# One four-tile burst for masked scores times values, in place of two two-tile bursts, in a vision-tower kernel

## The chip, the cores and the metric

The kernel runs on one core of one Trainium2 chip. The metric is device time in microseconds (us); lower is better. The engines are TensorE (PE, with its weight loads shown apart as PEld), VectorE (DVE), ScalarE (ACT), GpSimd (POOL) and SyncE (SP), which issues the DMAs. They run side by side and meet at semaphores.

## The reference

The input is `x` of shape (128, 64, 64, 64). Three stages follow one another:

- *Tokens.* Each 4x4 patch of pixels is averaged to one token of 64 channels; a small attention (8 heads) of that token over its 16 pixels is added.
- *Attention.* Linear attention with decay, 8 heads of width 8, in chunks of 128 tokens:

```
scores = einsum('bhcd,bhed->bhce', qi, ki) * mask
intra  = einsum('bhce,bhed->bhcd', scores, vi)
inter  = einsum('bhcd,bhde->bhce', qi * q_dec, S)
```

  `mask` is the decay matrix, zero above the diagonal, and `S` the state carried from one chunk to the next. The output is `intra + inter`, projected, added and normalised.
- *Experts.* A router chooses 2 of 8 small MLPs per token; their sum is added and normalised.

The change touches `intra` alone.

## The kernel before

Two images are laid side by side on the 128 partitions (64 channels each), and half of their pixels make one *unit*: 128 tokens of two images, so 16 (image, head) pairs in one tile of 128 x 128. There are 128 units. The first two stages are a software pipeline written out by hand: each engine runs a function `step(i, r)` for unit `4 i + r`, and a step works on several units at once, each at another stage (`there(i, r, lag)` says whether the unit `lag` steps back exists). The parity `s = r % 2` chooses one of two buffers, and the state `S` is used in odd steps alone. Most of the steps run in a hardware loop. Each engine executes its own list in program order; a `wait_ge` stops the list of its engine until a semaphore has the given count.

In one step TensorE computes, for the newest unit, four pixel rows each of keys (`keys(j)`, L342 and L347, tiles of 64x64) and values (`values(j)`, L366, whole array); for the unit one step back, sums over a head (`selected()`, L317 and L320, four column tiles of 128x32); for older units the projections and the attention. `queries()` (L377) and `queries_turned()` (L385) prepare the queries of the next unit; between them ScalarE (L568 to L584) and VectorE (L818 to L825) compute a norm. Everything here is f32, and one f32 matmul shows as two matmul records and two weight loads.

Attention of the unit four steps back: `scores(f)` (L412) computes queries times keys, for half `f` of the 16 pairs, into PSUM banks 3 and 4. VectorE multiplies them by the mask into `sm` (L763, masks 0 and 1 after `scores(0)`, masks 2 and 3 after `scores(1)`). `attend(f)` (L427) applies them to the values: the group `g` of four pairs goes to column tile `g` of the array, that is to partitions 32 g to 32 g + 31 of PSUM bank 7, and its four pairs add up there, because `vpad` holds each pair's values with zeros in the other pairs' columns. `attend(0)` handles groups 0 and 1, eight matmuls in the order jj outer, g inner, so that two column tiles take turns; `attend(1)` does groups 2 and 3 the same way at the end of the step. In odd steps L434 adds the state's part. Then `o_done` lets ScalarE evict the result (L529), and `attended()` (L455) of the next step projects it.

The wait functions matter for the order: `keys_free(j)` stands ahead of `keys(j)` and waits until VectorE (L752) and ScalarE (L517) have read the keys of row j - 1. ScalarE's list in the middle of a step is: L555 to L563 (values and tokens out of PSUM), `values(1)` (L524), L568 to L584. VectorE's is: L752 for row 1, L800 to L810, L818 to L825, L752 for row 2, the softmax steps L835 to L844, masks 2 and 3, L752 for row 3.

Of the kernel before, what the change touches and what calls it, by code (L numbers as in the profile page):

```python
# [13 lines left out]
def vit_tower_kernel(nc, x, ln_q_w, ln_q_b, Wq, ln_kv_w, ln_kv_b, Wkv, proj_w, proj_b,  # L14
                     w_qkv, w_proj, b_proj, slopes, router_w, w1, b1, w2, b2, out):
    P = 128
# [19 lines left out]
    def done(i, r, lag, per, plus=0):  # L36

        if isinstance(i, int):
            return max(0, max(0, min(UNITS, 4 * i + r - lag + 1)) * per + plus)
        return i * (4 * per) + (r - lag + 1) * per + plus  # L40

    def there(i, r, lag):
        return not isinstance(i, int) or 0 <= 4 * i + r - lag < UNITS

    def pairs(i, r, back, per=1):

        if isinstance(i, int):
            return max(0, min(UNITS // 2, 2 * i + r // 2 + back)) * per
        return i * (2 * per) + (r // 2 + back) * per
# [14 lines left out]
    def units(eng, step):  # L64

        step(-1, 2)
        step(-1, 3)
        for i in (0, 1):
            for r in range(4):
                step(i, r)  # L70
        with eng.Fori(2, UNITS // 4 - 1) as i:
            for r in range(4):
                step(i, r)
        for u in range(UNITS - 4, UNITS + 6):
            step(u // 4, u % 4)

    with ExitStack() as ctx:
# [3 lines left out]
        def sem(name):  # L81
            return ctx.enter_context(nc.semaphore(name))
# [10 lines left out]
        B7 = ps[:, 7, :]  # L93
# [27 lines left out]
        with ExitStack() as early:  # L121
            def sb1(name, shape, dt=F32):
                return early.enter_context(nc.sbuf_tensor(name, shape, dt))
# [57 lines left out]
            qdm = sb1("qdm", [P, P])  # L181
            sblk = sb1("sblk", [P, P])
# [49 lines left out]
            vk_ev = sem("vk_ev")  # L232
# [3 lines left out]
            sb_done = sem("sb_done")  # L236
            qd_done = sem("qd_done")
            qm_done = sem("qm_done")
            sc_done = sem("sc_done")
            mask_done = sem("mask_done")  # L240
            o_done = sem("o_done")
            oT_done = sem("oT_done")
            pr_done = sem("pr_done")
            lt_done = sem("lt_done")
# [51 lines left out]
            def _(pe):  # L296
# [8 lines left out]
                def step(i, r):  # L305
                    s = r % 2
# [45 lines left out]
                    def keys_free(j):  # L352

                        if there(i, r, 0):
                            if j == 0:
                                pe.wait_ge(x_in[r], 16 * NL * (i + 1))
                            pe.wait_ge(kq_done, done(i, r, 1, ST, j))
                            pe.wait_ge(cs_done, done(i, r, 1, ST, j))

                    def values(j):  # L360

                        if there(i, r, 0):
                            pe.wait_ge(vs_done, done(i, r, 1, ST, j))
                            xv = xb[:, r, :].rearrange("p (b t d) -> p b d t", b=ST, d=ST)
                            for b in range(ST):
                                mm = nc.tensor.matmul(VB[:, b * P:(b + 1) * P], xv[:, b, j], w_ckv[:, P:2 * P],  # L366
                                                      start=True, stop=True)
                            mm.then_inc(v_pe, 1)
# [43 lines left out]
                                nc.tensor.matmul(SCB[g % 2], kT[hp, s, :], qm[hp, s, :],  # L412
                                                 start=True, stop=True).then_inc(sc_done, 1)

                    def attend(f):

                        if not there(i, r, 4):
                            return
                        if f == 0:
                            pe.wait_ge(lt_done, done(i, r, 5, 1))  # L420
                            pe.wait_ge(sb_done, pairs(i, r, -2 + s))
                            pe.wait_ge(vk_ev, done(i, r, 4, 2))
                        pe.wait_ge(mask_done, done(i, r, 5, 4, 2 * f + 2))
                        for jj in range(4):
                            for g in (2 * f, 2 * f + 1):
                                at = g * 4 * VW + jj * W
                                mm = nc.tensor.matmul(B7[g * W:(g + 1) * W, 0:P], vpad[:, s, at:at + W],  # L427
                                                      sm[:, (4 * g + jj) * P:(4 * g + jj + 1) * P], start=(jj == 0),
                                                      stop=(jj == 3 and s == 0))
                        if f == 1:  # L430
                            if s == 1:

                                pe.wait_ge(qd_done, pairs(i, r, -1))
                                mm = nc.tensor.matmul(B7[:, 0:P], sblk[:], qdm[:], start=False, stop=True)  # L434
                            mm.then_inc(o_done, 1)

                    def aggregated():

# [6 lines left out]
                    def projected():  # L445
                        if there(i, r, 2):
                            pe.wait_ge(agT_ev, done(i, r, 2, 1))
                            nc.tensor.matmul(B6[:, P:2 * P], w_pj[:], aggT[:], start=True,
                                             stop=True).then_inc(pj_done, 1)
# [25 lines left out]
                    keys(1)  # L475
                    attn_vk()
                    values(1)
                    attend(0)
                    keys_free(2)
                    queries()  # L480
                    keys(2)
# [5 lines left out]
                    aggregated()  # L487
                    values(3)
                    projected()
                    attend(1)  # L490
                units(pe, step)

            @block.scalar
# [850 lines left out]
```

## Time and profile before

| | us |
|---|---|
| median of 3 runs | 3491.15 (3491.13 to 3492.43) |
| the profiled execution | 3490.56 |
| its span in the profile | 3488.5 |
| TensorE busy | 3308.4 (95%) |
| VectorE, GpSimd, ScalarE busy | 2025.1, 1746.6, 1488.5 |

The pipeline of the first two stages runs from about 46 us to about 2874 us, the routing and the experts after it. A time is the start of an instruction, counted from the start of the span. A row of the order of time merges neighbouring instructions of a line: its length goes from the first start to the last end. Matmuls overlap in that view, since a matmul's end is modelled, so the distance between starts of rows is what a group costs.

### The profile page before, as it was taken

The numbers are of one execution on the slowest core, as the hardware profiler recorded it, in microseconds if no ns is written. First come the engines' busy times: TensorE is split into PE (matmuls) and PEld (weight loads), VectorE is DVE, ScalarE is ACT, GpSimd is POOL, SyncE is SP. The second block draws the span as 40 slices with busy tenths as digits, with TensorE's granted clock in tenths as the row PEclk, the third lists the DMA queues.
The fourth block names the chain that finished last, engine by engine and source line by source line (L and its number), as shares of the span: only waits on it lengthen the run. The fifth ranks groups of instructions, "written<-read, shape, count | busy, mean of one in ns | idle before, by whom it ended". The sixth has DMA issues, their size and how long they took to land. (4 is left out here: it accounts for less than half of the span.)

```text
span 3488.5 us, 68919 instructions
## 1 busy us (share of the span) xinstructions
PE 3308.4 (95%) x21221; PEld 2063.2 (59%) x21221; DVE 2025.1 (58%) x4349; ACT 1488.5 (43%) x4493; POOL 1746.6 (50%) x1789
## 2 busy tenths in 40 slices
PE   4999999999999999999999999999999976399998
PEld 2666666666666666666666666666666646244333
DVE  3566666666666666666666666666666650655554
ACT  2444444444444444444444444444444433244443
POOL 2655555555555555555555555555555530011211
PEclk9999999999999999999999999999999975599999
DMA  3322222222222222222222222222222100000000
GB/s 65 61 50 49 48 48 48 48 48 48 48 48 48 48 48 48 48 48 48 48 48 48 48 48 48 48 48 48 48 48 48 25 1 5 0 19 18 18 21 21
DMA packets 573517, 144.09 MB, mean 41 GB/s; under 512 B 573472, under 2 KB 573472, under 8 KB 573472
## 3 DMA queue, kind: packets, MB, share of 16 engines
q1 hardware_dynamic: 573472, 143.51, 21.3%
q8 instruction: 25, 0.41, 0.1%
q14 instruction: 20, 0.16, 0.0%
HBM read 135.08 MB, written 8.39 MB: 41 GB/s over the span
## 5 line engine op out<-in xcount | busy, mean ns | idle before, releaser
L366 PEld LDWEIGHTS ps<-w_ckv,xb 128*128 128x128 f32 x4096 | 1008.2, 327 | 218.1 <-issue 192.1
L366 PE MATMUL ps<-w_ckv,xb 128*128 128x128 f32 x4096 | 1048.1, 399 | 0.9 <-DVE kqs L752 0.8
L636 POOL TENSOR_TENSOR pv<-vs,aw 128x512 f32<-128x512 f32 x512 | 534.7, 1077 | 668.5 <-DVE aw L854 365.8
L524 ACT ACTIVATE vs<-ps 128x512 f32<-128x512 f32 x512 | 305.7, 597 | 848.8 <-PE ps L366 848.8
L342 PE MATMUL ps<-xb,w_ckv 64*64 64x512 f32 x2048 | 553.4, 617 | 0.0
L347 PE MATMUL ps<-xb,w_ckv 64*64 64x512 f32 x2048 | 553.3, 617 | 0.0
L752 DVE TENSOR_TENSOR kqs<-ps,qqT 128x512 f32<-128x512 f32 x512 | 350.9, 685 | 332.9 <-PE ps L347 332.9
L763 DVE TENSOR_TENSOR sm<-ps,decay 128x512 f32<-128x512 f32 x512 | 328.7, 683 | 155.2 <-PE ps L412 155.2
L517 ACT ACTIVATE sqs<-ps 128x512 f32<-128x512 f32 x512 | 304.7, 595 | 211.8 <-PE ps L347 211.8
L666 POOL TENSOR_TENSOR xt<-xb 128x512 f32<-128x512 f32 x256 | 325.3, 1292 | 20.3 <-issue 19.9
L643 POOL TENSOR_TENSOR pv<-pv 128x512 f32<-128x512 f32 x256 | 323.1, 1284 | 0.0
L412 PE MATMUL ps<-qm,kT 32*128 32x512 f32 x1024 | 292.3, 647 | 0.0
L427 PE MATMUL ps<-sm,vpad 128*32 128x128 f32 x4096 | 278.0, 279 | 9.5 <-DVE sm L763 9.5
L656 POOL TENSOR_TENSOR htok<-htok,bp_row 128x128 f32<-128x128 f32 x128 | 58.3, 456 | 424.0 <-ACT htok L563 424.0
L1287 DVE TENSOR_TENSOR hid<-ps,hid 128x512 f32<-128x512 f32 x256 | 162.5, 685 | 156.2 <-PE ps L1080 150.4
L800 DVE TENSOR_REDUCE agg<-pv 128x128 f32<-128x1024 f32 x128 | 248.2, 1939 | 0.6 <-POOL pv L643 0.6
L427 PEld LDWEIGHTS ps<-sm,vpad 128*32 128x32 f32 x4096 | 207.8, 111 | 47.4 <-DVE sm L763 10.1
L1187 ACT ACTIVATE hid<-ps,b1p 128x1024 f32<-128x1024 f32 x128 | 142.5, 1114 | 195.8 <-PE ps L1069 195.8
L782 DVE TENSOR_TENSOR lt<-ps,htok 128x128 f32<-128x128 f32 x128 | 37.3, 291 | 272.0 <-PE ps L462 136.7
L818 DVE SCALAR_TENSOR_TENSOR ps<-ps,y0s 128x48 f32<-128x48 f32 x136 | 29.4, 216 | 275.6 <-ACT y0s L584 275.6
L977 POOL TENSOR_TENSOR y<-y 128x512 f32<-128x512 f32 x32 | 33.2, 1039 | 268.2 <-ACT y L1200 268.2
L669 POOL TENSOR_TENSOR xt<-xt 128x512 f32<-128x512 f32 x128 | 162.2, 1267 | 10.0
(222 smaller groups left out, 4899.9 us busy)
## 6 DMA issues: line engine op xcount, KB each, us to landing
xb<-in_x_dram SPq DMA_DIRECT2D x512, 256.0 KB, 4.3
out_dram<-outb SPq DMA_DIRECT2D x128, 64.0 KB, 1.6
w1p<-in_L_ffn_w_dram SPq DMA_DIRECT2D x16, 16.0 KB
b2v<-in_L_ffn_b_dram SPq DMA_DIRECT2D x16, 2.0 KB
w2p<-in_L_ffn_w_dram SPq DMA_DIRECT2D x8, 16.0 KB
b1p<-in_L_ffn_b_dram SPq DMA_DIRECT2D x8, 0.2 KB
sm<-in_L_tok_Wkv_dram SPq DMA_DIRECT2D x4, 16.0 KB, 2.0
w_avki<-in_L_attn_w_qkv_dram SPq DMA_DIRECT2D x4, 16.0 KB, 2.8
```

Source lines behind the costliest of these rows:

```text
L342: nc.tensor.matmul(KB[own, :], w_ckv[own, 2 * P + m * C:2 * P + (m + 1) * C], xv[own, j], start=True, stop=True)
L347: mm = nc.tensor.matmul(CB[(1 - m) * C:(2 - m) * C, :], w_ckv[own, m * C:(m + 1) * C], xv[own, j], start=True, stop=True)
L366: mm = nc.tensor.matmul(VB[:, b * P:(b + 1) * P], xv[:, b, j], w_ckv[:, P:2 * P], start=True, stop=True)
L412: nc.tensor.matmul(SCB[g % 2], kT[hp, s, :], qm[hp, s, :], start=True, stop=True).then_inc(sc_done, 1)
L427: mm = nc.tensor.matmul(B7[g * W:(g + 1) * W, 0:P], vpad[:, s, at:at + W], sm[:, (4 * g + jj) * P:(4 * g + jj + 1) * P], start=(jj == 0), ...
L517: nc.scalar.activation(sqs[:, j, :], CB, ACT.Square).then_inc(cs_done, 1)
L524: nc.scalar.activation(vs[:, s, j * 4 * P:(j + 1) * 4 * P], VB, ACT.Copy).then_inc(vs_done, 1)
L636: nc.gpsimd.tensor_tensor(pv[:, at].rearrange("p (k d) -> p k d", d=D), vs[:, s, at].rearrange("p (k d) -> p k d", d=D), aw[:, j * W4:(j + ...
L643: nc.gpsimd.tensor_tensor(pv[:, j * 4 * P:(j + 1) * 4 * P], pv[:, j * 4 * P:(j + 1) * 4 * P], pv[:, (j + 2) * 4 * P:(j + 3) * 4 * P], ALU. ...
L666: ins = nc.gpsimd.tensor_tensor(xt[:, h * H:(h + 1) * H], xb[:, f, h * H:(h + 1) * H], xb[:, f, (h + 2) * H:(h + 3) * H], ALU.add)
L752: V.tensor_tensor(kqs[:, j, :].rearrange("p (t d) -> p t d", d=ST), KB.rearrange("p (t d) -> p t d", d=ST), qqT[:, s, :].unsqueeze(2).to_b ...
L763: V.tensor_tensor(sm[:, g * 512:(g + 1) * 512].rearrange("p (h c) -> p h c", c=P), SCB[g % 2].rearrange("p (h c) -> p h c", c=P), decay[:, ...
```

## The change

`attend(f)` becomes `attend()`. It issues all sixteen matmuls in one burst, at the place of the old `attend(1)`, in the order jj outer, g inner, so that four column tiles take turns. The call between `values(1)` and `keys_free(2)` goes away. The wait for `sb_done` is now made in odd steps only, ahead of L434. Operands, shapes, addresses and the sums themselves stay.

```diff
-                    def attend(f):
+                    def attend():
 
                         if not there(i, r, 4):
                             return
-                        if f == 0:
-                            pe.wait_ge(lt_done, done(i, r, 5, 1))
-                            pe.wait_ge(sb_done, pairs(i, r, -2 + s))
-                            pe.wait_ge(vk_ev, done(i, r, 4, 2))
-                        pe.wait_ge(mask_done, done(i, r, 5, 4, 2 * f + 2))
+                        pe.wait_ge(lt_done, done(i, r, 5, 1))
+                        pe.wait_ge(vk_ev, done(i, r, 4, 2))
+                        pe.wait_ge(mask_done, done(i, r, 5, 4, 4))
                         for jj in range(4):
-                            for g in (2 * f, 2 * f + 1):
+                            for g in range(4):
                                 at = g * 4 * VW + jj * W
                                 mm = nc.tensor.matmul(B7[g * W:(g + 1) * W, 0:P], vpad[:, s, at:at + W],
                                                       sm[:, (4 * g + jj) * P:(4 * g + jj + 1) * P], start=(jj == 0),
                                                       stop=(jj == 3 and s == 0))
-                        if f == 1:
-                            if s == 1:
+                        if s == 1:
 
-                                pe.wait_ge(qd_done, pairs(i, r, -1))
-                                mm = nc.tensor.matmul(B7[:, 0:P], sblk[:], qdm[:], start=False, stop=True)
-                            mm.then_inc(o_done, 1)
+                            pe.wait_ge(sb_done, pairs(i, r, -2 + s))
+                            pe.wait_ge(qd_done, pairs(i, r, -1))
+                            mm = nc.tensor.matmul(B7[:, 0:P], sblk[:], qdm[:], start=False, stop=True)
+                        mm.then_inc(o_done, 1)
...
                     values(1)
-                    attend(0)
                     keys_free(2)
...
                     projected()
-                    attend(1)
+                    attend()
```

## Rows read from the trace of the kernel before

**Rows 1.** The page: busy time by engine, and the group of L427.
```profile
PE 3308.4 (95%) x21221; PEld 2063.2 (59%) x21221; DVE 2025.1 (58%) x4349; ACT 1488.5 (43%) x4493; POOL 1746.6 (50%) x1789
...
L427 PE MATMUL ps<-sm,vpad 128*32 128x128 f32 x4096 | 278.0, 279 | 9.5 <-DVE sm L763 9.5
```
**Rows 2.** Stages: window, its length, busy us (instructions) by engine, granted clock, DMA.
```profile
1534.04:1535.04 1.00, 1.00 (x23) 1.00 (x26) 0.91 (x3) 0.56 (x1) 0.59 (x1) 1.00 0.00 0
...
1513.55:1513.65 0.10, 0.10 (x5) 0.10 (x8) 0.00 (x0) 0.00 (x0) 0.10 (x1) 1.00 0.62 143
137.60:2770.00 2632.40, 2632.40 (x17194) 1703.91 (x17197) 1620.26 (x3454) 1163.04 (x3874) 1567.00 (x1574) 1.00 0.25 48
...
1503.91:1525.81 21.90, 21.90 (x144) 14.07 (x142) 13.51 (x29) 9.44 (x31) 13.24 (x14) 1.00 0.25 48
1525.81:1547.40 21.59, 21.59 (x145) 14.07 (x143) 13.22 (x30) 9.77 (x33) 12.66 (x14) 1.00 0.25 49
```
**Rows 3.** TensorE in order of time, an odd step: start us, length us.
```profile
1501.08 1.90 PE L366 MATMUL ps<-w_ckv,xb 128*128 128x128 f32 x8
1502.91 1.07 PE L427 MATMUL ps<-sm,vpad 128*32 128x128 f32 x16
1503.91 0.70 PE L377 MATMUL ps<-w_qc,red 128*128 128x256 f32 x2
1504.54 0.65 PE L342 MATMUL ps<-xb,w_ckv 64*64 64x512 f32 x2
...
1505.56 1.13 PE L412 MATMUL ps<-qm,kT 32*128 32x512 f32 x4
1506.62 2.13 PE L366 MATMUL ps<-w_ckv,xb 128*128 128x128 f32 x8
1508.59 0.27 PE L385 MATMUL ps<-ident,q 128*128 128x128 f32 x1
...
1512.13 1.07 PE L427 MATMUL ps<-sm,vpad 128*32 128x128 f32 x16
```
**Rows 4.** TensorE in order of time, in the ramp, before attention has begun.
```profile
112.52 1.90 PE L366 MATMUL ps<-w_ckv,xb 128*128 128x128 f32 x8
114.25 0.60 PE L377 MATMUL ps<-w_qc,red 128*128 128x256 f32 x2
114.78 0.65 PE L342 MATMUL ps<-xb,w_ckv 64*64 64x512 f32 x2
...
118.76 0.33 PE L385 MATMUL ps<-ident,q 128*128 128x128 f32 x1 [0.82 <-DVE kqs L752]
```
**Rows 5.** TensorE in order of time: four column tiles, and one whole-array tile.
```profile
1513.55 1.06 PE L317 MATMUL ps<-kqs,selk 128*32 128x512 f32 x8
...
3207.72 1.08 PE L1088 MATMUL ps<-tokT,centre 128*128 128x512 f32 x2
```
**Rows 6.** TensorE in order of time, end of an even step.
```profile
1534.04 0.74 PE L427 MATMUL ps<-sm,vpad 128*32 128x128 f32 x10
1534.52 0.62 PE L317 MATMUL ps<-kqs,selk 128*32 128x512 f32 x2
...
1536.76 0.49 PE L455 MATMUL ps<-w_ap,oT 128*128 128x128 f32 x2
```
**Rows 7.** ScalarE and VectorE in order of time, the same odd step.
```profile
1503.02 0.60 ACT L524 ACTIVATE vs<-ps 128x512 f32<-128x512 f32 x1 [0.95 <-PE ps L366]
1504.64 0.28 ACT L568 ACTIVATE qps<-ps 128x128 f32<-128x128 f32 x1 [1.03 <-PE ps L377]
...
1507.79 0.68 DVE L752 TENSOR_TENSOR kqs<-ps,qqT 128x512 f32<-128x512 f32 x1
...
1510.38 1.28 DVE L763 TENSOR_TENSOR sm<-ps,decay 128x512 f32<-128x512 f32 x2
```
**Rows 8.** TensorE in order of time, in the drain.
```profile
2849.49 1.92 PE L427 MATMUL ps<-sm,vpad 128*32 128x128 f32 x16
2851.34 2.08 PE L412 MATMUL ps<-qm,kT 32*128 32x512 f32 x4
```

## The prediction

> **What bounds the kernel now.** Read the busy line first: TensorE is busy 95% of the span, twice any DMA share and well above VectorE's 58% [rows 1]. A busy TensorE can still be waiting, because matmul ends are modelled, so I went to the stages next. From 137.6 to 2770 us its busy time equals the window, at granted clock 1.00, and VectorE, ScalarE and GpSimd stand at 62%, 44% and 60% [rows 2]. Two neighbouring steps take 21.90 and 21.59 us; each has about 144 matmul records and as many weight loads, two records per f32 matmul [rows 2]. Then the order of time inside a step: each group of matmuls starts where the one before ends, with no idle time named in front of it [rows 3]. So in 124 of the 128 steps with an `attend` pair TensorE's own work sets the pace, and what is cut there comes off the span, until an engine that feeds it becomes late.
>
> **What a burst costs.** The 4096 records of L427 are 256 bursts of 16, two per unit [rows 1]. A burst's row is 1.07 us long and one record lasts 0.27 us, so first and last start lie 0.80 us apart. The burst goes round two column tiles, so a tile starts 8 records in 0.80 us: one about every 0.11 us, first included. The two tiles run beside each other. The question of the change is whether four do.
>
> The nearest rows say yes. L317 goes round four column tiles of the same shape of weights (128x32) with 512 columns in place of 128: its 8 records take 1.06 us from the first start to the last end [rows 5]. L1088, one tile of the whole array with 512 columns, takes 1.08 us for 2 records [rows 5]. Eight on four tiles cost what two cost on one, so all four stream at once. A round of L427 at four tiles is then taken as long as at two, 0.11 us, plus a stagger of about 0.01 us for the two added tiles. New burst: 0.81 us between first and last start, with twice the matmuls. Bounds: 0.80 us (no stagger at all) from below, 1.6 us (each record still costs 0.80/15 = 0.053 us, as at two tiles, 31 intervals) from above. I take 0.81 because L317 is the nearest row in tiles and type; the 1.6 us stays for the range.
>
> **The change part by part.**
> 1. *The first burst goes from between `values(1)` and `queries()`.* Now L427 starts at 1502.91, L377 at 1503.91 and the next `keys` (L342) at 1504.54 [rows 3]. L366's eight records start at 1501.08 in the same step, 3.46 us ahead of that L342, and 1.83 us ahead of L427. The trace of before holds the form of after too: in the ramp, before the first unit has reached attention, L366 is followed directly by L377. There L366 starts at 112.52, L377 at 114.25, L342 at 114.78: 2.26 us [rows 4]. Ramp form: 1.73 us from L366 to L377 and 0.53 from L377 to L342. Present form: 1.83 + 1.00, and 0.63. The edit saves (1.83 + 1.00 + 0.63) - 2.26 = 1.20 us per step. Of it 0.80 is the burst, the rest are the two changes of the tile shape around it, and a weight load of L377 that the end of L366 hides. Nothing covers or uncovers this; both forms are on record at full clock.
> 2. *Its eight matmuls go into the last burst.* +0.01 us by the working above. In an even step the old last burst used tiles 2 and 3 only, and L317 of the next step already starts 0.48 us into it [rows 6]. That could have been an overlap that the change loses. It isn't: tiles 2 and 3 must run 8 records and then their share of L317 and L320, and only their end counts; tiles 0 and 1 just finish earlier. With four tiles full, the longest tile does the same work. So 0 lost; the other bound is 0.4 us (the whole head start lost), in even steps alone, 0.2 us per step on average.
> 3. *Waits.* `sb_done` is now waited for only ahead of L434, in odd steps. The VectorE multiply that gives it follows `lt` near the start of a step, some 10 us earlier: 0. The merged wait for `mask_done` is the one that the second burst had: masks 2 and 3 end at 10.38 + 1.28 = 1511.66, and L427 starts at 1512.13 [rows 3, 7], 0.47 us of slack. Behind that wait stand L434 and the next step's `selected()`, as now: 0.
> 4. *What is late next.* The removed 1.20 us were cover for whatever runs from the first half of a step into the second. The tight one is the chain behind `queries()`: L377, ScalarE L568 to L584, VectorE L818 to L752, then L385, which stands behind `keys_free(3)`. Now L752 ends at 1507.79 + 0.68 = 1508.47 and L385 starts at 1508.59 [rows 3, 7]: only 0.12 us, about what a wait takes to pass. The matmuls between L377 and L385 stay, so this distance only shrinks by the 0.10 us of item 1 on both sides. But L568 also follows ScalarE's eviction L524, which ends at 1503.02 + 0.60 = 1503.62, while L568, at 1504.64 now, would be due at 1503.44 [rows 7]. It will be some 0.1 us late, in an odd step, where the chain is longest. The ramp shows such a wait: L385 with 0.82 us idle in front, for VectorE L752 [rows 4], in a step that lacks the `scores(1)` of a full step, 1.06 us from L412 at 1505.56 to L366 at 1506.62 [rows 3]: 0.82 is less than 1.06, so it confirms that the chain nearly fits. I take 0.05 us per step; bounds 0 and 0.3 us (VectorE and ScalarE slowed by each other's nearness as well).
>    The other engines have 21.6 us for 13.5, 12.7 to 13.2 and 9.8 us of work [rows 2] and can follow a step of 20.6. The x loads need a quarter of the DMA time [rows 2].
>
> Per full step: 1.20 - 0.01 - 0.05 = 1.14 us. Times 124: 141.4 us. The last four pairs lie in the drain at half clock or behind VectorE. Two of them (one from 2849.49 to 2851.34 [rows 8]) have the burst of 1.85 us ahead of `scores(1)` on the path, so 3.7 us; two wait for VectorE's long chain anyway, 0. **Sum:** 145 us. The profiled execution takes 3490.56 us (span 3488.5), 0.6 below the median of the runs shown: 3490.6 - 145 = 3345.5, as a median 3346 us. The stages after 2874 us don't change.
>
> **The rivals.**
> *A. The instructions come too slowly.* The burst is now 32 matmul records and 32 weight loads that should start in 0.81 us, 13 ns each. The fullest microsecond of the trace, 1534.04 to 1535.04, has 22 to 23 matmuls and 26 loads starting [rows 2], 20 ns each. If 20 ns is a limit, the burst lasts 1.3 us: +0.5 per step, 3346 + 62 = 3408. If a record costs 0.053 us as at two tiles, +0.8 per step: 3449. For it: no stretch with 128 columns on four tiles exists. Against: within 1513.55 to 1513.65 four tiles start 8 loads and 4 to 5 matmuls in 0.1 us [rows 2], so at least in the short the pace is there, and in the 1534 window tiles 0 and 1 were occupied by L317's long records, so that work and not supply limited the count. Chance 0.10.
> The Trainium skill, page "TensorE: Matmul & The Clock Gate", section "Wait — 56ns, not 53.3ns?", states that with hardware decode off the sequencer spends about 62 ns on each matmul, which binds where the array needs less. By that rule 32 records would take 1.98 us, an estimate from the page, and the time would come to about 3490; the two-tile burst with its 53 ns per record [rows 3] is a little faster than the rule allows, though a filled queue could explain that.
> *B. The cover is missing more than I think.* The chain of item 4 stops L385 for 0.3 us per step: 3346 + 37 = 3383. For it: 0.12 us of slack [rows 3, 7]. Against: ramp steps whose idle time is below what `scores(1)` fills. Chance 0.07.
> *C. Slower.* Half of the doubled burst (32 instructions, what a burst needs today) is ready in the queue, the others arrive at the mean pace of a step, 286 in 21.90 us or 77 ns each [rows 2]. The burst then takes 0.44 + 32 x 0.077 = 2.9 us, 2.1 more than now, against 1.20 saved: +0.9 per step, 3490.6 + 112 = about 3600. The sign turns where an instruction needs more than (0.81 + 1.14 - 0.44)/32, or 47 ns. The 1534 window with 20 ns speaks against it. Chance 0.03.
>
> **How the numbers follow.** Forecast 0.80, A 0.10, B 0.07, C 0.03. The forecast's own range is 3336 (no stall, the drain a little shorter) to 3364 (0.15 us per step left behind somewhere). With B and the milder half of A the range is 3336 to 3400. About 0.2% (7 us) is what this kernel's runs can tell from nothing: faster by more 0.95, within it 0.02 (a pace between A's worst and C's), slower 0.03.
>
> **What would show each step.** Right: L427 with 128 bursts of 32 records, first to last start 0.8 us; L366 followed by L377 1.73 us after its start in every step; step lengths of about 20.4 and 20.75 us; L385 with at most 0.1 us idle, behind VectorE L752. A shows as a longer L427 row at the same count; B as idle time at L385 or L342 with VectorE or ScalarE as the releaser; a lost overlap as a longer way from L427 to L455 in even steps (now 2.72 us, from 1534.04 to 1536.76 [rows 6]). The prediction is wrong if steps don't shorten by more than 1 us though TensorE keeps its full clock.

## The result and the profile after

The changed kernel takes 3358.89 us (median of 4 runs, 3357.21 to 3360.96) against 3491.14 us for the kernel before on the same chip: ratio 0.9622, 95% interval 0.9605 to 0.9638. The forecast was 3346 us, range 3336 to 3400 us: right in sign and range, 13 us too low. All the kernels below were timed beside the kernel before, whose medians (3491.14, 3490.50 and 3490.51 us) agree within 0.7 us, so their times can be compared with each other. The profiled execution took 3357.21 us, span 3355.2. Line numbers after the edit are two or three lower than before (L427 is L425, L752 is L749, L825 is L822); those up to L412 stay.

The page of the changed kernel, its busy line and the group of the burst:

```profile
PE 3167.0 (94%) x21221; PEld 1953.0 (58%) x21221; DVE 2052.1 (61%) x4349; ACT 1474.8 (44%) x4493; POOL 1748.5 (52%) x1789
...
L425 PE MATMUL ps<-sm,vpad 128*32 128x128 f32 x4096 | 141.8, 280 | 7.4 <-DVE sm L760 7.4
```

The records are as many as before [rows 1], each as long (280 against 279 ns), and yet the group's busy time is half: 141.8 for 278.0 us. Busy time counts a moment once, so twice as many records now lie on top of each other.

The stages, with the columns of rows 2:

```profile
137.60:2640.00 2502.40, 2497.16 (x17167) 1596.50 (x17166) 1642.86 (x3440) 1148.43 (x3871) 1567.44 (x1571) 1.00 0.26 50
1498.04:1518.68 20.64, 20.61 (x143) 13.23 (x143) 13.54 (x30) 9.66 (x33) 12.69 (x14) 1.00 0.27 51
1518.68:1539.40 20.72, 20.72 (x143) 13.20 (x143) 13.73 (x29) 9.33 (x31) 13.27 (x14) 1.00 0.26 51
```

The first short window runs from L377 of an even step to the next L377, the second is the odd step after it. The even step took 21.59 us [rows 2] and takes 20.64 now, the odd one took 21.90 and takes 20.72. In the even step TensorE is no longer busy all the time (20.61 of 20.64). VectorE's busy time there has grown from 13.22 us [rows 2] to 13.54 with no instruction added, which is the hint to what follows.

TensorE in order of time: the second half of an even step with its burst, then the same of the odd step after it:

```profile
1500.65 2.13 PE L366 MATMUL ps<-w_ckv,xb 128*128 128x128 f32 x8
1502.81 0.33 PE L385 MATMUL ps<-ident,q 128*128 128x128 f32 x1
1503.07 0.65 PE L342 MATMUL ps<-xb,w_ckv 64*64 64x512 f32 x2
...
1506.41 1.08 PE L425 MATMUL ps<-sm,vpad 128*32 128x128 f32 x32
1507.31 1.04 PE L317 MATMUL ps<-kqs,selk 128*32 128x512 f32 x8
...
1509.14 0.49 PE L453 MATMUL ps<-w_ap,oT 128*128 128x128 f32 x2
...
1516.94 1.90 PE L366 MATMUL ps<-w_ckv,xb 128*128 128x128 f32 x8
1518.68 0.60 PE L377 MATMUL ps<-w_qc,red 128*128 128x256 f32 x2
1519.21 0.65 PE L342 MATMUL ps<-xb,w_ckv 64*64 64x512 f32 x2
...
1521.29 2.13 PE L366 MATMUL ps<-w_ckv,xb 128*128 128x128 f32 x8
1523.26 0.27 PE L385 MATMUL ps<-ident,q 128*128 128x128 f32 x1
1523.46 0.65 PE L342 MATMUL ps<-xb,w_ckv 64*64 64x512 f32 x2
...
1526.81 1.08 PE L425 MATMUL ps<-sm,vpad 128*32 128x128 f32 x32
1527.82 0.49 PE L432 MATMUL ps<-qdm,sblk 128*128 128x128 f32 x2
```

Three things are to be seen. The burst has 32 records in a row of 1.08 us, where 16 took 1.07 [rows 3]. L366 to L377 to L342 takes 1.74 + 0.53 us, the form that the ramp showed [rows 4]. And L385 follows L366 after 1.97 us in the odd step, but after 2.16 us in the even one, and L342 another 0.26 in place of 0.20 us later. The same holds over the steady part of the trace. The even steps take 20.64 and 20.75 us in turns, where experiment 1 below has 20.39, so they lose 0.25 or 0.36 us; the odd ones take 20.72 us and lose nothing. That is 0.153 us per step. The forecast had named 20.4 and 20.75 us: the odd step came as forecast, the even one did not.

What L385 waits for, in the group of its weight loads (idle time and releaser at the end), in the kernel before (137.6 to 2770 us) and after (137.6 to 2640 us):

```profile
L385 PEld LDWEIGHTS ps<-ident,q 128*128 128x128 f32 x122 | 23.1, 190 | 0.0
```
```profile
L385 PEld LDWEIGHTS ps<-ident,q 128*128 128x128 f32 x120 | 16.6, 138 | 16.7 <-DVE kqs L749 16.7
```

Two explanations were set against each other. Theory P: VectorE's multiply that makes q2 (L822) now meets an addition of GpSimd. Theory S: ScalarE's part of the chain (L565 to L581) starts too late behind its eviction L521.

### The profile page after: what moved, and what is told of

Read it like the earlier page. It is cut to its first block and busy times, and to the rows that moved or that the text cites. A ratio compares the mean times of both kernels' runs of the same rounds, so it can differ in the third digit from the quotient of the medians.

```text
span 3355.2 us, 68942 instructions
## 1 busy us (share of the span) xinstructions
PE 3167.0 (94%) x21221; PEld 1953.0 (58%) x21221; DVE 2052.1 (61%) x4349; ACT 1474.8 (44%) x4493; POOL 1748.5 (52%) x1789
## 5 line engine op out<-in xcount | busy, mean ns | idle before, releaser
L366 PEld LDWEIGHTS ps<-w_ckv,xb 128*128 128x128 f32 x4096 | 1008.0, 327 | 217.0 <-issue 189.7
L366 PE MATMUL ps<-w_ckv,xb 128*128 128x128 f32 x4096 | 1047.9, 399 | 0.9 <-DVE kqs L749 0.8
L521 ACT ACTIVATE vs<-ps 128x512 f32<-128x512 f32 x512 | 305.7, 597 | 839.4 <-PE ps L366 839.4
L749 DVE TENSOR_TENSOR kqs<-ps,qqT 128x512 f32<-128x512 f32 x512 | 350.6, 685 | 330.6 <-PE ps L347 330.6
L342 PE MATMUL ps<-xb,w_ckv 64*64 64x512 f32 x2048 | 552.1, 616 | 0.0
L663 POOL TENSOR_TENSOR xt<-xb 128x512 f32<-128x512 f32 x256 | 325.4, 1292 | 20.4 <-issue 20.0
L412 PE MATMUL ps<-qm,kT 32*128 32x512 f32 x1024 | 292.3, 647 | 2.9 <-DVE sm L760 2.2
L530 ACT ACTIVATE ssb<-ps 128x512 f32<-128x512 f32 x128 | 76.4, 597 | 194.5 <-PE ps L320 194.5
L342 PEld LDWEIGHTS ps<-xb,w_ckv 64*64 64x64 f32 x2048 | 99.8, 131 | 92.9 <-issue 46.4
L425 PE MATMUL ps<-sm,vpad 128*32 128x128 f32 x4096 | 141.8, 280 | 7.4 <-DVE sm L760 7.4
```

Of the source, the lines that this page charges most:

```text
L342: nc.tensor.matmul(KB[own, :], w_ckv[own, 2 * P + m * C:2 * P + (m + 1) * C], xv[own, j], start=True, stop=True)
L412: nc.tensor.matmul(SCB[g % 2], kT[hp, s, :], qm[hp, s, :], start=True, stop=True).then_inc(sc_done, 1)
L521: nc.scalar.activation(vs[:, s, j * 4 * P:(j + 1) * 4 * P], VB, ACT.Copy).then_inc(vs_done, 1)
L663: ins = nc.gpsimd.tensor_tensor(xt[:, h * H:(h + 1) * H], xb[:, f, h * H:(h + 1) * H], xb[:, f, (h + 2) * H:(h + 3) * H], ALU.add)
L749: V.tensor_tensor(kqs[:, j, :].rearrange("p (t d) -> p t d", d=ST), KB.rearrange("p (t d) -> p t d", d=ST), qqT[:, s, :].unsqueeze(2).to_b ...
```

## The experiments

All are variants of the changed kernel, but the last, which is one of the kernel before; times are medians, ratios against the kernel before.

**1. GpSimd's order.** The additions of x go ahead of the one on `htok`; the last of them, `red`, stays where it was.

```diff
-                        pool.wait_ge(vk_ev, done(i, r, 3, 2))
-                        nc.gpsimd.tensor_tensor(htok[:, o, :], ..., ALU.add).then_inc(hb_done, 1)
                     if there(i, r, -2):
...
                         link(nc.gpsimd.tensor_tensor(xp[:, 0:2, :], xp[:, 0:2, :], xp[:, 2:4, :], ALU.add))
+                    if there(i, r, 3):
+                        pool.wait_ge(vk_ev, done(i, r, 3, 2))
+                        nc.gpsimd.tensor_tensor(htok[:, o, :], ..., ALU.add).then_inc(hb_done, 1)
+                    if there(i, r, -2):
                         pool.wait_ge(qp_pe, done(i, r, -1, 1))
```

> The changed kernel, with GpSimd's additions of x moved ahead of its addition on htok; red stays last. Theory P (port): in the changed kernel VectorE's multiply that makes q2 (L822) meets GpSimd's L668 in the even steps and takes 0.82 us in place of 0.42 us, so L385 starts 0.26 to 0.37 us late there, 0.155 us per step. With GpSimd done before q2 begins, L822 should take 0.42 us in both parities, L385 should follow L366 after 0.23 us, a step takes 20.56 us, and the time is 3358.9 - 19 = 3340 us. Rival S (ScalarE): the chain is late because L565 follows the eviction L521 more closely than before; then L385 stays late and the time stays at 3359 us.

Measured: 3340.17 us (3338.69 to 3342.10), ratio 0.9569 (0.9553 to 0.9584), as theory P had it to within a microsecond. VectorE and GpSimd in order of time in an even step of the changed kernel, then the same with TensorE in an even step of this one:

```profile
1501.34 0.82 DVE L822 TENSOR_SCALAR q<-qps,yrs 128x64 f32<-128x64 f32 x2
1502.08 0.68 DVE L749 TENSOR_TENSOR kqs<-ps,qqT 128x512 f32<-128x512 f32 x1
...
1501.40 0.71 POOL L668 TENSOR_TENSOR xt<-xt 128x256 f32<-128x256 f32 x1
```
```profile
1534.20 0.42 DVE L824 TENSOR_SCALAR q<-qps,yrs 128x64 f32<-128x64 f32 x2
...
1530.30 0.67 POOL L665 TENSOR_TENSOR xt<-xt 128x256 f32<-128x256 f32 x1
1531.05 0.46 POOL L668 TENSOR_TENSOR htok<-htok,bp_row 128x128 f32<-128x128 f32 x1
1532.62 0.41 POOL L673 TENSOR_TENSOR red<-xt 128x128 f32<-128x128 f32 x1 [1.11 <-ACT h L570]
...
1533.43 2.13 PE L366 MATMUL ps<-w_ckv,xb 128*128 128x128 f32 x8
1535.40 0.27 PE L385 MATMUL ps<-ident,q 128*128 128x128 f32 x1
```

In the changed kernel q2's two small multiplies overlap GpSimd's L668 and end 0.05 us after it, at 1502.16; with GpSimd out of the way they take half the time, and L385 is back at 1.97 us behind L366, in all even steps. Theory S is out: ScalarE's L565 starts 0.69 to 0.77 us after L377 in the changed kernel and in this one alike, and the stall is there in the one and gone in the other. The group of L385's weight loads has lost its idle time:

```profile
L385 PEld LDWEIGHTS ps<-ident,q 128*128 128x128 f32 x120 | 23.9, 199 | 0.0
```

The same multiply, mean ns of one of its two instructions, in the steady stage of before, changed, experiment 1:

```profile
L825 DVE TENSOR_SCALAR q<-qps,yrs 128x64 f32<-128x64 f32 x244 | 63.8, 303 | 4.4
```
```profile
L822 DVE TENSOR_SCALAR q<-qps,yrs 128x64 f32<-128x64 f32 x240 | 80.7, 378 | 4.3
```
```profile
L824 DVE TENSOR_SCALAR q<-qps,yrs 128x64 f32<-128x64 f32 x240 | 50.2, 252 | 4.3
```

The move takes other meetings away too. VectorE's multiply for `kd`, which runs in odd steps beside GpSimd's first additions of x, falls from 1.35 us to 0.28:

```profile
L809 DVE TENSOR_TENSOR kd<-kpl,kdec 128x128 f32<-128x128 f32 x60 | 16.7, 278 | 0.0
```

This does not bear on the even steps, which have no such multiply; in the one shown VectorE had idled 1.74 us for ScalarE ahead of the chain.

**2. VectorE's order.** The third row of keys goes ahead of the chain that makes q2.

```diff
+                    keys(2)
                     link, n = chain(dve, newt_ch, (4 * i + r + 2) * 3)
...
                         ins.then_inc(q2_done, 1)
-                    keys(2)
```

> The changed kernel, with VectorE's product of the third row of keys (L749) moved ahead of the chain L815 to L822, into the 1.74 us in which VectorE now waits for ScalarE in even steps. L385 waits for both. Theory P and any theory in which the chain up to L749 is too long: in even steps q2 ends 0.68 us sooner counted to L385, so L385 is no longer late although L822 may still meet GpSimd; in odd steps L749 then ends when it did. 3340 us (3338 to 3345). If it was not this chain that held L385: 3359 us.

Measured: 3356.33 us (3355.64 to 3356.94), ratio 0.9614 (0.9598 to 0.9630): a miss by 16 us. The expectation held for the even steps and failed for the odd ones. TensorE in this kernel, an even step and the next odd one, then VectorE and GpSimd in the odd one:

```profile
1499.54 2.13 PE L366 MATMUL ps<-w_ckv,xb 128*128 128x128 f32 x8
1501.51 0.27 PE L385 MATMUL ps<-ident,q 128*128 128x128 f32 x1
...
1519.92 2.13 PE L366 MATMUL ps<-w_ckv,xb 128*128 128x128 f32 x8
1522.14 0.30 PE L385 MATMUL ps<-ident,q 128*128 128x128 f32 x1
...
1518.39 1.35 DVE L807 TENSOR_TENSOR kd<-kpl,kdec 128x128 f32<-128x128 f32 x1
1519.67 0.68 DVE L749 TENSOR_TENSOR kqs<-ps,qqT 128x512 f32<-128x512 f32 x1
...
1521.00 0.89 DVE L823 TENSOR_SCALAR q<-qps,yrs 128x64 f32<-128x64 f32 x2
...
1521.03 0.65 POOL L668 TENSOR_TENSOR xt<-xt 128x256 f32<-128x256 f32 x1
```

In an odd step VectorE has no free time there (L807 runs until 1519.74), so the moved product only pushes q2 later, into GpSimd's L668: L823 takes 0.89 us, and L385 comes 2.22 us after L366. L807 itself is long because it runs beside GpSimd (0.28 us in experiment 1). The stall has changed parity: an even step now takes 20.39 us and an odd one 21.00, so 0.31 us lost in even steps have become 0.27 us in odd ones.

**3. ScalarE's order.** `values(1)` goes behind the chain that ends with `y0s`.

```diff
-                    values(1)
                     if there(i, r, -1):
...
                     nc.scalar.activation(y0s[:], y0[:], ACT.Square).then_inc(rs_ch, 1)
+                    values(1)
                     centred(2)
```

> The changed kernel, with ScalarE's eviction values(1) (L521) moved behind the chain L565 to L581. Rival S: L565 starts as soon as L377 ends and L385 is no longer late, 3340 us. Theory P: L565 gains at most 0.1 us (it starts 0.70 us after L377, and 0.66 at best in the ramp), which shifts q2 by 0.1 us against GpSimd; L822 still meets L666 or L668 and the stall stays in the main: 3350 to 3362 us.

Measured: 3411.31 us (3406.80 to 3413.13), ratio 0.9770 (0.9754 to 0.9787), outside both expectations. The eviction now comes too late for `values(2)`, here in an odd step:

```profile
1509.96 1.13 PE L412 MATMUL ps<-qm,kT 32*128 32x512 f32 x4
1511.42 2.13 PE L366 MATMUL ps<-w_ckv,xb 128*128 128x128 f32 x8 [0.33 <-ACT vs L521]
1513.39 0.27 PE L385 MATMUL ps<-ident,q 128*128 128x128 f32 x1
```

L366 starts 0.4 us later than the 1.06 us after L412 that it needs, and L385, now reached later, no longer waits. So this run does not tell the two theories apart; experiment 1 does. It shows that the step has a second place with little cover. Against experiment 1 it costs 71 us. Most steps are 0.4 to 0.5 us longer, some 52 us in 124. Another 15 us come from TensorE's clock: 14 of the steps took 21.8 to 22.2 us, and in each of them the granted clock fell to 0.5 (1.2 GHz) for a stretch (mean 0.92 over the step), as it does in no steady step of the changed kernel or of experiment 1. In one of them, 1486.48 to 1508.41, TensorE had idled 0.41 us ahead of L366 before the clock fell at 1491.5. Why these 14 steps and not the others, which idle there too, no run shows.

**4. Both moves, 1 and 2.**

> Both the GpSimd move and the VectorE move. If either alone removes the wait before L385, both together give the same, 3340 us, since TensorE then has no wait left: L385 follows L366 after 0.23 us in every step and a step takes 20.56 us. A further gain of over 3 us would show a wait that the profile does not name.

Measured: 3339.91 us (3339.40 to 3340.52), ratio 0.9568 (0.9552 to 0.9584), the same as experiment 1. With GpSimd's additions out of the way, VectorE's order is worth nothing.

**5. One burst, two tiles at a time.** The place stays, the order of the two old bursts comes back.

```diff
-                        for jj in range(4):
-                            for g in range(4):
+                        for g0, jj in [(0, 0), (0, 1), (0, 2), (0, 3), (2, 0), (2, 1), (2, 2), (2, 3)]:
+                            for g in (g0, g0 + 1):
```

> The changed kernel with one burst at the same place, but in the order of the two old bursts: first the eight matmuls of groups 0 and 1 in turns, then the eight of groups 2 and 3. This is the kernel before with its first burst moved, and without four tiles in turns. Theory T (tiles run side by side only where their instructions stand near each other in the list): in the kernel before L317 on tiles 0 and 1 began when 10 of the 32 instructions of a burst on tiles 2 and 3 were still to start, 0.47 us into it. So the second half starts 0.47 us after the first, the burst lasts about 1.27 us from first to last start in place of 0.81, a step gets 0.46 us longer: 3358.9 + 57 = 3416 us. Rival N (no overlap over a longer distance than the neighbour): 1.7 us, +0.87 us per step, 3467 us. Rival F (TensorE sorts freely within its queue, or the whole gain came from the removed changes of tile shape): no difference, 3359 us.

Measured: 3417.65 us (3414.22 to 3418.19), ratio 0.9792 (0.9775 to 0.9808). Theory T (tiles run side by side only where their instructions stand near each other in the list) holds within 2 us; N (no overlap over a distance) and F (TensorE sorts freely, or the gain was the tile shapes) are out.

**6. One tile at a time.** `for g in range(4):` outside, `for jj in range(4):` inside.

> The changed kernel with the sixteen matmuls in the order g outer, jj inner: four matmuls (8 records) on one column tile, then the next tile. If the distance that TensorE looks ahead is some 10 instructions (5 records), the next tile starts after 3 records or 0.33 us: 1.8 us from first to last start, +1.0 us per step, about 3485 us. If it is 5 instructions of the same tile: 0.47 us each, 2.2 us, 3535 us. With no looking ahead at all: 31 x 0.109 = 3.4 us, +2.6 us, about 3680 us. If TensorE sorts freely: 3359 us.

Measured: 3533.67 us (two runs, 3533.54 and 3533.79), ratio 1.0127 (1.0107 to 1.0148): 1.3% slower than before, with the same instructions as the changed kernel. Of the cases in the expectation, the one with 5 instructions of the same tile had said 3535 us. The burst in an odd step of experiment 5 and of experiment 6:

```profile
1516.65 1.54 PE L425 MATMUL ps<-sm,vpad 128*32 128x128 f32 x32
1518.12 0.49 PE L432 MATMUL ps<-qdm,sblk 128*128 128x128 f32 x2
```
```profile
1533.07 2.46 PE L425 MATMUL ps<-sm,vpad 128*32 128x128 f32 x32
1535.46 0.49 PE L432 MATMUL ps<-qdm,sblk 128*128 128x128 f32 x2
```

Less the last record's 0.27 us, the same 32 records start within 0.81, 1.27 and 2.19 us in the orders of four, two and one tile: 0.80 us for the eight records of a tile, plus 0, 1 or 3 hops of 0.46 us.

**7. The kernel before with GpSimd's order of experiment 1.**

> The kernel before the change, with GpSimd's additions of x moved as in the first experiment. There the first burst stands between values(1) and queries(), and no step waits at L385 (it follows L366 after 0.23 us in all steady steps), so taking the meeting of VectorE and GpSimd away should gain nothing: 3490 us, within 2 us. If GpSimd's order is worth 19 us by itself, whatever the burst does, it comes to 3472 us.

Measured: 3488.42 us (3482.30 to 3490.98), ratio 0.9995 (0.9985 to 1.0004): nothing. The 19 us of experiment 1 exist only once the first burst is gone.

## Why the prediction was right, and 13 us off

*Item 1, the removed burst: right.* The ramp's form came as it stood. Where no stall is left (experiment 1) a step takes 20.56 us on average against 21.74, so 1.18 us are saved, of 1.20 - 0.01 forecast.

*Item 2, four tiles: right.* 0.81 us from first to last start. In even steps L425 to L453 takes 2.73 us (forecast: 2.72, nothing lost). Experiment 5 prices the four tiles in turns by themselves: 59 us of the 132 gained. The rest is the move. It saves the two shape changes (0.40 us per step, by item 1), lets the two halves overlap (1.27 us for what took 0.80 twice), and loses the stall (0.15): 0.58 us per step, or 72 us.

*Item 3, waits: right as far as shown.* The burst has 7.4 us of idle time named in the whole run, as little as before [rows 1].

*Item 4, what is late next: the right place, the wrong size and the wrong reason.* The forecast named the chain L377, L568, L818, L752, L385 and took "0.05 us per step; bounds 0 and 0.3 us"; it measured 0.153 us. 0.10 us more in 124 steps is 12.8 us, nearly the whole distance from 3346 to 3358.9. The check from the other side: the forecast without this term is 3346 - 6 = 3340 us, and experiment 1 took 3340.17. The step that was wrong is the reason: "It will be some 0.1 us late, in an odd step, where the chain is longest". The odd step lost nothing; the even one did. Nor did ScalarE's eviction hold up the chain. L568 starts 0.73 to 0.81 us after L377 in the kernel before, and its successor L565 0.69 to 0.77 us after it now:

```profile
1498.24 0.60 ACT L521 ACTIVATE vs<-ps 128x512 f32<-128x512 f32 x1 [1.29 <-PE ps L366]
1498.74 0.27 ACT L565 ACTIVATE qps<-ps 128x128 f32<-128x128 f32 x1
```

The forecast moved the chain as a rigid piece. But q2's multiply moved against GpSimd's additions, which hang on the earlier `htok`: it had started at 1529.23 in an even step of before, just as GpSimd's last addition ended, and now runs beside L668. The Trainium skill, page "SBUF — State Buffer", section "Who interferes with whom", states that a tensor_scalar of VectorE can take the port pair that it shares with GpSimd, and that whoever comes second waits for the whole instruction. The trace agrees with the waiting (the pair of multiplies ends 0.05 us behind L668 and takes 0.82 us, 0.42 alone). Who comes second can't be read from the starts: in the odd step of experiment 2 the first multiply started 0.03 us ahead of L668 and was the one that took longer. No run here tells the ports from another cause of the same meeting.

*Rivals.* A (instructions come too slowly) is out: 32 loads and 32 matmuls started in 0.81 us, 13 ns each, where the fullest microsecond of before had 20 ns. The Trainium skill, page "TensorE: Matmul & The Clock Gate", section "Wait — 56ns, not 53.3ns?", states about 62 ns per matmul with hardware decode off, which the prediction priced at about 3490 us. The 32 matmul records here started 25 ns apart on average, so that bound did not act. Whether it is absent or a filled queue hid it, no run shows. B (the chain stops L385 for 0.3 us per step) happened at half its size. Its price was 6 us too high, since the forecast that it adds to already had 0.05 of the 0.3 us. C is out with A. From the last L377 to the end of the span 4.2 us are gained, where the forecast had 3.7 us for two bursts of the drain.

## What to carry to other kernels

The small matmuls on column tiles here cost what the longest tile costs, if the list goes round the tiles (0.81 us for 32 records); the same instructions tile after tile took 2.7 times as long (2.19 us). When a block is taken out of a saturated engine's list, compare the trace's own form without it (a ramp or a drain often has one) for the saving, and then look at what now coincides: here a chain on VectorE slid against GpSimd's work, and a meeting on engines that were busy 61% and 52% of the span became the new bound. The cure was GpSimd's order, and it is worth nothing in the kernel that still has the cover.

## What the runs showed of the hardware that was not expected

A later matmul starts ahead of an earlier one when it is for another column tile and the busy tile has come near the end of its records. In the kernel before L317 begins 0.48 us into a burst on two other tiles [rows 6], and L427 goes on behind it:

```profile
1534.61 0.50 PE L427 MATMUL ps<-sm,vpad 128*32 128x128 f32 x6
```

In experiments 5 and 6 each hop to the next tile costs the same, 0.46 to 0.47 us, whether the waiting group is one tile wide or two. At that moment the busy tile has started five of its eight records and has three left; with two tiles running that is six left in all, with one tile three. So the look-ahead does not go by a count over all tiles. Whether it goes by the three left or by the five started can't be told, since every tile had eight records in every order. Which tile a record belongs to is taken from the kernel's order, as the trace doesn't name it. The Trainium skill, page "TensorE: Matmul & The Clock Gate", section "The mechanism", holds that matmuls start and end strictly in program order; for the starts, the records here say otherwise.
